# A second buffer for the transposed q and k, an MLP sum in two halves, later group steps, and the scaled identities on GpSimd

## What is computed

```python
ada = t_emb @ w_ada + b_ada
sh_msa, sc_msa, g_msa, sh_mlp, sc_mlp, g_mlp = jnp.split(ada, 6, axis=-1)
xm = expmap0(layer_norm(logmap0(x)) * (1 + sc_msa) + sh_msa)
q = _to_heads(plin(xm, w_q, b_q)); k = ...; v = ...   # plin(x, w, b) = expmap0(logmap0(x) @ w + b)
attn = softmax(einsum('bhqd,bhkd->bhqk', logmap0(q), logmap0(k)) / sqrt(HD))
out_h = expmap0(einsum('bhqk,bhkd->bhqd', attn, logmap0(v)))
x = mobius_add(x, expmap0(g_msa * logmap0(plin(_from_heads(out_h), w_o, b_o))))
xm = expmap0(layer_norm(logmap0(x)) * (1 + sc_mlp) + sh_mlp)
ff = plin(plin(xm, w_f1, b_f1), w_f2, b_f2)
return x_in + mobius_add(x, expmap0(g_mlp * logmap0(ff)))
```

## Time and profile before

| | us |
|---|---|
| median of 3 runs | 774.34 (772.27 to 775.95) |
| the profiled execution, whole | 778.25 |
| its span | 776.2 |
| TensorE busy (matmuls) | 650.5 |
| VectorE busy | 657.1 |
| ScalarE busy | 521.6 |
| GpSimd busy | 341.3 |

### The profile page before, as it was taken

How to read it: one execution, slowest core, us unless ns; L and a number is a source line. 1 busy time by engine, 2 the same in 40 slices (tenths; PEclk the granted TensorE clock), 3 DMA queues, 4 the chain that set the end, 5 groups by cost and what they waited for, 6 DMA issues and landing times. The chain is left out here.

```text
span 776.2 us, 27058 instructions
## 1 busy us (share of the span) xinstructions
PE 650.5 (84%) x8419; PEld 466.0 (60%) x8433; DVE 657.1 (85%) x2171; ACT 521.6 (67%) x1563; POOL 341.3 (44%) x683
## 2 busy tenths in 40 slices
PE   4956889999999998999999997506869999999996
PEld 2645667777777776777677775403336656656664
DVE  1877789999999999999999996586898998998975
ACT  1123567777777777777777775335768888888884
POOL 1002556666666666666666664111243233323321
PEclk9978799999999999999999998557899999999999
DMA  9942576666676666666666664313435445545523
GB/s 320 358 114 63 123 141 136 152 137 148 135 147 142 143 140 145 137 147 134 147 133 141 143 130 97 71 39 97 125 91 150 148 125 163 155 121 160 163 71 108
DMA packets 184804, 107.50 MB, mean 138 GB/s; under 512 B 140188, under 2 KB 167591, under 8 KB 184744
## 3 DMA queue, kind: packets, MB, share of 16 engines
q1 hardware_dynamic: 182952, 103.99, 54.5%
q10 hardware_dynamic: 1792, 2.89, 1.0%
HBM read 64.11 MB, written 9.18 MB: 94 GB/s over the span
## 5 line engine op out<-in xcount | busy, mean ns | idle before, releaser
L875 PE MATMUL p_qkv<-wqkv,tT 128*128 128x256 f32 x768 | 198.2, 396 | 5.5 <-DVE u L1129 5.5
L875 PEld LDWEIGHTS p_qkv<-wqkv,tT 128*128 128x128 f32 x768 | 140.0, 195 | 23.0 <-issue 6.3
L889 PEld LDWEIGHTS p_o<-v,pT 64*64 64x64 f32 x4096 | 67.3, 137 | 22.2 <-issue 22.2
L889 PE MATMUL p_o<-v,pT 64*64 64x17 f32 x4096 | 73.6, 210 | 0.0
L497 POOL TENSOR_TENSOR rt<-ss,c_mhalf 128x2 f32<-128x2 f32 x32 | 23.9, 747 | 106.2 <-ACT wqkv L700 106.2
L848 PE MATMUL p_oz<-wo,oT 128*128 128x256 f32 x256 | 69.7, 397 | 0.0
L438 POOL TENSOR_TENSOR rt<-ss_t,c_mhalf 128x1 f32<-128x1 f32 x64 | 42.1, 658 | 60.6 <-ACT junk L627 53.7
L652 ACT ACTIVATE pT<-p_s 128x1024 f32<-128x1024 f32 x64 | 65.5, 1023 | 3.0 <-PE p_s L865 1.9
L1129 DVE SCALAR_TENSOR_TENSOR u<-p_qkv,ct,bqkv 128x768 f32<-128x768 f32 x64 | 64.3, 1005 | 3.4 <-PE p_qkv L875 3.4
L610 ACT ACTIVATE oT<-p_oz 128x256 f32<-128x256 f32 x64 | 24.5, 383 | 56.6 <-PE p_oz L840 56.6
L937 PE MATMUL p_qkv<-wff,qk 128*128 128x384 f32 (+1 forms) x128 | 58.9, 608 | 3.7 <-ACT qk L712 3.6
(11 more groups left out here) (273 smaller groups left out, 1672.4 us busy)
## 6 DMA issues: line engine op xcount, KB each, us to landing
mod<-mod_rows SPq DMA_DIRECT2D x128, 128.0 KB, 2.9
x_all<-in_x SPq DMA_DIRECT2D x8, 1024.0 KB, 14.1
gate<-mod_rows SPq DMA_DIRECT2D x128, 64.0 KB, 2.7
mod<-mod_rows SPq DMA_DIRECT2D x32, 256.0 KB, 4.2
mod_b<-mod_rows SPq DMA_DIRECT2D x32, 256.0 KB, 4.4
out<-x_all SPq DMA_DIRECT2D x32, 256.0 KB, 3.0
gate<-gate_rows SPq DMA_DIRECT2D x32, 128.0 KB, 2.9
bqkv<-gate_rows SPq DMA_DIRECT2D x32, 128.0 KB, 2.9
```

The lines of the kernel that those rows point to most:

```text
L875: mm = pe.matmul(p_qkv[:, a * D:a * D + D], tT[:, k, c, :], wqkv[:, c, a * D:a * D + D], start=c == 0, stop=c == C - 1)
L889: mm = pe.matmul(p_o[S * e:S * e + S, col:col + VW], pT[keys, e, g, :], v[keys, k, 2 * g + e, :], start=True, stop=True, skip_group_check= ...
```

## The change

In the attention stage the transposed q and k get a second buffer in the last four tiles of `g_all`. The transpose and TensorE's scores take the buffer by the tile's parity, with a semaphore each, and the transpose no longer waits for the scores of the tile before; the last tile writes the first buffer and keeps that wait. VectorE's gating of the last four tiles, which writes over the second buffer, waits for the scores of tile 61.

In the MLP stage three things change. The scaled identities are made by GpSimd, as the first thing of its slot, by `tensor_tensor` with the factor's column broadcast; ScalarE makes none. TensorE's sum is split by the tile of the pair: the first half stands before the transposes, the second half between the transposes and the products. And the group's steps stand later: `output_norms` behind the slot's last VectorE step, `output_root` behind the shifts, ScalarE's tanh behind the squares L700.

```diff
@@ buffers and SyncE
+        qkTs = (qkT[:, :, :, :], g_all[:, T - 4:T, :].rearrange("p t d -> p (t d)").bitcast(F16).rearrange(
+            "p (a g n) -> p a g n", a=2, g=G))
...
                     sp.wait_ge(again_ready, 2 * i + 2)
-                    after(sp, s_psum, i)
+                    if last_tile(h, off, L_H):
+                        sp.wait_ge(s_psum, i)
                     sp.sem_inc(rows_begun, 1)
...
@@ GpSimd
+            def diagonals(i, k, q, col, g):
+
+                pool.wait_ge(al2_ready, g + 1)
+                pool.wait_ge(be2_ready, g + 1)
+                after(pool, out_psum, i - 1)
+                for j in range(2):
+                    for n, fac2 in enumerate((al2, be2)):
+                        pool.tensor_tensor(diags[k][j][n], ident[:, :], fac2[:, q, col + j:col + j + 1].broadcast_to([P, P]),
+                                           ALU.mult).then_inc(diag_ready, 1)
...
@@ ScalarE, slot2
-                        act.activation(diags[k][j][n], ident[:, :], ACT.Copy, scale=fac2[:, q, col + j:col + j + 1]).then_inc(diag_ready, 1)
...
@@ TensorE, slot2
                 if on_sum(h, off, M_O):
-                    add_up(slots - M_O, (off - M_O) % 2, (off - M_O) % TURN)
+                    add_up(slots - M_O, 0, (off - M_O) % 2, (off - M_O) % TURN)
                 if on2(h, off, M_Q):
                     i, k = slots - M_Q, (off - M_Q) % 2
                     transpose_t2(i, k)
+                if on_sum(h, off, M_O):
+                    add_up(slots - M_O, 1, (off - M_O) % 2, (off - M_O) % TURN)
...
@@ VectorE, gate_z
+                if i >= T - 4:
+                    dve.wait_ge(s_psum, T - 2)
...
@@ VectorE, slot2
-                if group_at(h, off, M_N) is not None:
-                    output_norms(group_at(h, off, M_N), parity(off, M_N))
+                if group_at(h, off, M_P) is not None:
+                    output_root(group_at(h, off, M_P))
...
```

More of the change, by code:

```diff
@@ L235, in build @@
         qk_ready = sem("qk_ready"); high_ready = sem("high_ready"); low_ready = sem("low_ready"); again_ready = sem("again_ready"); v_ready = sem("v_ready")
-        rows_begun = sem("rows_begun"); qkT_in = sem("qkT_in")
+        rows_begun = sem("rows_begun"); qkT_in = [sem(f"qkT_in{k}") for k in range(2)]
         s_psum = sem("s_psum"); p_ready = sem("p_ready")
@@ L322, in at_start, with last_tile @@
             return isinstance(h, int) and h == 0 and off == 0
+        def last_tile(h, off, lag):
+            return isinstance(h, int) and 2 * h + off - lag == T - 1
         def on2(h, off, lag):
@@ L462, in scale_v, with low_parts @@
                                    fac[:, 2 * H:3 * H].unsqueeze(2).broadcast_to([P, H, HD]), ALU.mult).then_inc(v_ready, 1)
-            def low_parts(i, k):
+            def low_parts(i, k, half):
                 pool.wait_ge(high_ready, i + 1)
                 pool.wait_ge(qk_ready, 2 * i + 2)
-                after(pool, qkT_in, 16 * (i - 1))
+                after(pool, qkT_in[k], 16 * half)
                 big = qk4s[k]
@@ L849, in project_o, with scores_wait, scores @@
                 mm.then_inc(z_psum, 1)
-            def scores_wait(i):
-                pe.wait_ge(qkT_in, 16 * i + 16)
+            def scores_wait(i, k, half):
+                pe.wait_ge(qkT_in[k], 16 * half + 16)
                 after(pe, p_ready, i)
-            def scores(i):
+            def scores(i, rows_of):
                 for g in range(G):
@@ L864, in scores @@
                             col = 512 * e + S * g
-                            mm = pe.matmul(p_s[tok, col:col + S], qkT[rows, 1, g, tok], qkT[rows, 0, g, tok], start=True, stop=True,
+                            mm = pe.matmul(p_s[tok, col:col + S], rows_of[rows, 1, g, tok], rows_of[rows, 0, g, tok], start=True, stop=True,
                                            skip_group_check=True)
@@ L939, in inner, with add_up @@
                 mm.then_inc(ff_psum, 1)
[L941 to L952 removed]
+            def add_up(i, j, k, r):
+                pe.wait_ge(diag_ready, 4 * i + 2 * j + 2)
+                if j == 0:
+                    pe.wait_ge(fg_ready, 2 * i + 2)
+                    after(pe, out_ready, i - 1)
+                acc = s_bank[2 + k][:, j * D:j * D + D]
+                xt, x1 = (big[:, bass.ds(2 * i + j, 1), :].rearrange("p a d -> p (a d)") for big in (x_all, g_all))
+                pe.matmul(acc, ident[:, :], xt, start=True, stop=False)
+                pe.matmul(acc, diags[k][j][0], x1, start=False, stop=False)
+                mm = pe.matmul(acc, diags[k][j][1], fgs[r][:, j, :], start=False, stop=True)
+                if j == 1:
+                    mm.then_inc(out_psum, 1)
             def slot2(h, off):
@@ L1479, in slot2 @@
                         dot_x1(i, j, r, q, col)
+                if group_at(h, off, M_N) is not None:
+                    output_norms(group_at(h, off, M_N), parity(off, M_N))
                 if group_at(h, off, M_P) is not None:
```

52 lines of the change are left out of this document (17 added, 35 removed).

## The result

The change made the kernel slower by 0.8%: 780.52 us median (779.71 to 783.02) against 774.34, a ratio of 1.0081 with a 95% interval of 1.0057 to 1.0106. The forecast was 770.4 us, faster: it missed by 10 us and in the sign, though its range of 761.5 to 781.0 just takes in the time.

A forecast was written before the change was run, and what follows sets the result against it. No engine but GpSimd had a tenth to spare, so only loops' idle time could be won. Attention -6.0, MLP +1.5, tail +0.5 made -4.0: 774.25 us from the profiled 778.25, 770.4 as median, range 761.5 to 781.

The forecast's parts named there:

- Two buffers: Attention stage: transposes no longer wait for scores, so mod and the stage's end come earlier; -6 us, from -1 to -9.
- ScalarE's loop 6.62: MLP plain slots: ScalarE's loop falls from 6.98 to 6.62 us, with a 0.7 wait for the second half-sum.
- A scaling on GpSimd 0.36: MLP stage: one 128 x 128 identity scaling on GpSimd takes 0.36 us, pitch 0.34, four 1.4.
- Contention, 4 x 0.16 behind the norms: Slot behind the norms: GpSimd's four scalings cost VectorE 0.16 us each, about 0.8 a group with the root held back.
- rival at full price: MLP stage: each GpSimd scaling costs VectorE 0.36 us; groups of 30.7, median 782.6; chance 22%.
- `rh` late by 0.35: Slot behind the norms: GpSimd's root for the next factors comes about 0.35 us late for VectorE, once a group.
- A group of 29.0: MLP stage: four slots take 28.2 us without contention plus 0.8 for it, 29.0 against 28.8 before.
- +1.5 for the MLP stage: MLP stage: 0.2 us more per group over 7.25 groups, +1.5 us.
- section on identities and the split: MLP stage: part of the prediction working out slot and group times with identities on GpSimd and the sum split; 28.2 without contention.
- Tail +0.5: Kernel's end: the last pair's GpSimd scalings meet VectorE's own sums, +0.5 us.
- The range: Whole kernel: from the no-contention time with a better first stage, 761.5 us, to just short of full price, 781.

The follow-up runs named there:

- e1: Kernel before with only the second buffer for transposed q and k, MLP stage as before: 768.6 us against 773.8, ratio 0.9930.
- e12: Changed kernel with one q and k buffer again and the wait for the scores back: 781.8 us, ratio 1.0121 to the kernel before.
- e9: The changed kernel, unaltered, measured again beside three of the experiments: 780.0 us against 772.3 for the kernel before, ratio 1.0106.
- e4: Changed kernel plus five unread TensorE products between first half-sum and transposes in the slot behind the factors: 774.2 us, ratio 0.9999 to the kernel before.
- e10: Changed kernel plus two unread TensorE products between first half-sum and transposes behind the factors: 773.3 us, ratio 1.0018 to the kernel before.
- e2: Changed kernel with the sum whole again before the transposes in every slot: 775.1 us, ratio 1.0012 to the kernel before.
- e5: Changed kernel with the scaled identities back on ScalarE, sum still split, group steps still late: 767.9 us, ratio 0.9960 to the kernel before.
- e6: Changed kernel with the group steps back in their old, earlier places: 771.0 us, ratio 0.9981 to the kernel before.
- e7: Changed kernel with the sum whole behind the factors, and GpSimd making rh before the identities behind the norms: 769.7 us, ratio 0.9967 to the kernel before.

## Why the prediction was wrong

Step by step, by the forecast's own terms:

- **Two buffers, -6 (-1 to -9).** -7.3 in the traces, -5.4 in e1, -1.9 between e12 and e9. The sign and the range held; the size is not settled. The forecast read an execution 3.9 us over its median, took that excess off as a whole at the end, and did not ask whether it sat in the very waits that it counted as gain.
- **ScalarE's loop 6.62, with a wait of 0.7.** 6.62 and 0.70.
- **A scaling on GpSimd 0.36, pitch 0.34.** 0.40 and 0.36 where nothing is in its way.
- **Contention, 4 x 0.16 behind the norms.** 4 x 0.15 (a pitch of 0.55 for 0.40). The Trainium skill, SBUF — State Buffer, section Who interferes with whom, calls the ports that the two engines share an exclusive lock. The rows show both engines slowed, and not a whole scaling of 0.40 lost each time, so the rival at full price fell.
- **`rh` late by 0.35.** 0.57.
- **A group of 29.0.** 29.05 to 29.08 (one group of 29.16 in e4 and in e10), wherever the order was this and the clock stayed up. The number is mostly no luck: VectorE's slots in e10 are 6.61 + 6.12, 6.79 and 9.54, where the forecast's terms make 12.75 for the first two, 6.6, and 9.65. Only in the last do two errors cancel (the late root 0.57 for 0.35, the contention 0.6 for 0.8).
- **+1.5 for the MLP stage.** This is the step that failed, and it failed at one place of the section on identities and the split: from the sentence that behind the factors' slot L707 follows VectorE by 0.2, the working went on with TensorE at full speed. It asked when TensorE's products would end in that slot and never how long TensorE would stand before it. The order on TensorE in front of the prediction already shows it: only three of six sum products are left between the last products and the transposes, so 1.3 us of cover is gone (e2, with the sum whole, stands 1.00 and not 2.33). The 0.4 by which e2's wait is longer than the 0.57 of before goes with the shorter slots around it, as far as the runs show. The clock's fall made 5.7 us in four groups and 2.0 in the last slots, 7.7 together. Profile against profile, the forecast was 774.25 and the execution took 781.65, 7.4 more: 7.7 for the clock, 1.2 for the rest of the tail, less 1.3 that the first stage gave beyond its -6 and 0.2 outside the span. The other 2.7 of the 10.1 us between forecast and median come from the excess of the profiled execution: 3.9 before, 1.1 now.
- **Tail +0.5.** +3.7 in the traces. With the gap filled (e4) it takes 28.4 us from the last row scaling to the end, before 26.7, changed 30.4: 2.0 are the clock, and 1.7 are there at full clock. Of those 1.7 both edits have a part: with the sum whole it is 27.6 (e2), with the identities on ScalarE 27.2 (e5). The forecast had only 0.5, for contention in the last sums.
- **The range.** By the forecast's own terms its lower end should be 760.9 (774.3 - 9 - 4.4), not 761.5. Nothing hangs on it.

The rival at full price gave 30.7 us a group and 782.6, close to what was measured (30.5 and 780.5), by a cause that was not there: e4 keeps all of the contention and is 6 us faster. It is an example of a number that comes out right for the wrong reason.

A view that would have shown it: the earlier trace rows give TensorE 0.26 of idle in a plain slot, so any wait that the change collects in one slot stands alone, and the granted clock falls from 1.00 to 0.50 at the end of the attention stage, where the forecast itself wrote of it. A rival "the clock falls in the MLP stage" belonged on the list.

## What to carry to other kernels

When work is moved on TensorE, look at what filled its longest wait, not only at what fills the loop: a filler that leaves that place can cost the clock for the work behind it, several times what the move was to bring. When three edits each shift a wait toward the same place, leave out one at a time: here the clock stayed up whenever one of the three was missing. And a number of one profile that lies over the median of the runs should be spread over the stages only after a second look, since the excess can sit in the very waits that the change is to remove.

## What the runs showed of the hardware that was not expected

- TensorE's clock fell to 0.50 after it had stood 2.33 us in an otherwise full stage (TensorE busy 92 of 100 us), behind five of the six such waits from 599 on. Where it stood 1.45 to 1.57 us (e6, e10) it did not fall. The length of the wait alone does not decide, though. The first of the six, as long as the others (2.33 before 599.36), left the clock at 1.00, in the changed kernel, e9 and e12 alike. And in the first slots of the stage, waits of 2.09 us before 568.34 (e5) and 568.67 (e7) left it at 1.00, while waits of 2.06 to 2.08 in the same place of the order (before 570.15 in the changed kernel, 569.91 in e10) had a fall to 0.50 behind them. What tells these apart stays open.
- Filling the wait with products that nobody reads was worth 6 to 7 us (e4: 780.5 to 774.2; e10: 780.0 to 773.3).
- GpSimd's two-input scaling and VectorE's two-input instructions stretch each other: 0.54 to 0.58 for 0.40, and 0.62 for 0.48. Small instructions are stretched as well: behind the factors, beside GpSimd's scalings, VectorE's `hh` of 128 x 2 takes 0.41, elsewhere 0.23:

```profile
658.73 0.40 POOL L530 TENSOR_TENSOR o<-ident,al 128x128 f32<-128x128 f32 x1
658.74 0.41 DVE L1368 TENSOR_SCALAR hh<-qf,bb 128x2 f32<-128x2 f32 x1
...
666.54 0.23 DVE L1368 TENSOR_SCALAR hh<-qf,bb 128x2 f32<-128x2 f32 x1
```
